# Attention in halves of float16: the low parts of the probabilities against the values' high part alone, two key tiles side by side in TensorE's column halves

## Time and profile before

| | us |
|---|---|
| median of 3 runs | 1426.91 (1426.64 to 1427.55) |
| span of the profiled execution, first to last instruction | 1425.4 |
| busy: PE / PEld / DVE / ACT / POOL | 1318.0 / 838.4 / 1147.2 / 1116.3 / 873.7 |

### The profile page before, as it was taken

The page is one execution under the profiler, slowest core; times in us unless marked ns, Lnnn a source line. Parts: engine busy times, 40 slices in busy tenths (PEclk is TensorE's granted clock), DMA queues, the critical chain, the costliest instruction groups (busy, mean ns, idle before and its releaser), DMA issues. The chain is left out here.

```text
span 1425.4 us, 25329 instructions
## 1 busy us (share of the span) xinstructions
PE 1318.0 (92%) x7328; PEld 838.4 (59%) x7328; DVE 1147.2 (80%) x3062; ACT 1116.3 (78%) x2327; POOL 873.7 (61%) x905
## 2 busy tenths in 40 slices
PE   4689999999999999999999999999999999898886
PEld 2456565665656565665656565666656566565554
DVE  4578887878887888878887888878788787887976
ACT  4768878788888888788887878788887888787664
POOL 1266667386645766386646766387646767786565
PEclk9799999999999999999999999999999999999998
DMA  6101111011101211021101211021100211210002
GB/s 199 27 20 38 64 30 31 27 57 45 37 21 45 59 29 31 23 60 44 36 24 26 72 35 31 23 60 43 38 24 23 75 35 37 61 42 27 18 33 85
DMA packets 45163, 61.82 MB, mean 43 GB/s; under 512 B 10464, under 2 KB 27104, under 8 KB 45024
## 3 DMA queue, kind: packets, MB, share of 16 engines
q1 hardware_dynamic: 45024, 60.20, 14.3%
HBM read 34.74 MB, written 4.46 MB: 27 GB/s over the span
## 5 line engine op out<-in xcount | busy, mean ns | idle before, releaser
L1100 DVE SCALAR_TENSOR_TENSOR prob_lo<-t,prob_hi 128x512 f16<-128x512 f32 x576 | 394.7, 686 | 76.0 <-ACT prob_hi L797 72.2
L797 ACT ACTIVATE prob_hi<-t 128x512 f16<-128x512 f32 x576 | 340.2, 591 | 146.1 <-PE t L1221 140.8
L1165 PE MATMUL s<-k_t,q_t 128*128 128x512 f32 (+3 forms) x1536 | 428.2, 383 | 23.8 <-DVE neg_max L1009 8.5
L829 ACT ACTIVATE prob<-prob,neg_max 128x896 f32<-128x896 f32 (+7 forms) x512 | 392.0, 767 | 7.2 <-DVE neg_max L1009 4.3
L1221 PE MATMUL t<-ident,prob 128*128 128x128 f32 x2304 | 350.8, 275 | 6.9 <-ACT prob L829 6.8
L1221 PEld LDWEIGHTS t<-ident,prob 128*128 128x128 f32 x2304 | 290.6, 143 | 109.7 <-ACT prob L829 13.2
L1009 DVE CUSTOM_DVE_ANT_0 prob<-s,mask 128x512 f32<-128x512 f32 (+3 forms) x512 | 289.6, 583 | 53.4 <-PE s L1165 33.3
L1165 PEld LDWEIGHTS s<-k_t,q_t 128*128 128x128 f32 x1536 | 244.9, 193 | 66.4 <-DVE neg_max L1009 19.0
L1136 PE MATMUL ot<-prob_lo,v_sb 128*128 128x512 f16 x576 | 221.0, 384 | 27.1 <-DVE prob_lo L1100 27.0
L1134 PE MATMUL ot<-prob_hi,v_sb 128*128 128x512 f16 x576 | 223.9, 389 | 0.9 <-DVE o_raw L1081 0.9
L770 POOL TENSOR_TENSOR o_lo<-o_raw,o_hi 128x256 f16<-128x256 f32 x128 | 86.2, 674 | 198.7 <-ACT o_hi L907 196.9
(11 more groups left out here) (106 smaller groups left out, 1841.4 us busy)
## 6 DMA issues: line engine op xcount, KB each, us to landing
swapped<-flat SPq DMA_DIRECT2D x320, 64.0 KB, 2.0
spread<-recip_rows SPq DMA_DIRECT2D x128, 128.0 KB
recip_rows<-turned SPq DMA_DIRECT2D x512, 0.5 KB
raw<-L_attn_w_in SPq DMA_DIRECT2D x8, 768.0 KB, 4.2
raw<-L_attn_w_out SPq DMA_DIRECT2D x8, 512.0 KB, 3.6
out<-acc SPq DMA_DIRECT2D x16, 256.0 KB, 2.0
acc<-L_attn_x SPq DMA_DIRECT2D x3, 1024.0 KB, 10.4
acc<-L_attn_x SPq DMA_DIRECT2D x4, 256.0 KB, 4.2
```

The lines of the kernel that those rows point to most:

```text
L797: act.activation(prob_hi[:, u % 2, :], t_ps[u % 2][:, :], ACT.Copy, scale=P_SCALE).then_inc(prob_hi_done, 1)
L829: act.activation(row, row, ACT.Exp, bias=neg_max[:, kk % 4, h:h + 1], scale=-1.0, accum_out=total[:, kk % 4, h:h + 1]).then_inc(ex_done, 1)
L1100: dve.scalar_tensor_tensor(out=prob_lo[:, u % 2, :], in0=t_ps[u % 2][:, :], scalar=P_SCALE, in1=prob_hi[:, u % 2, :], op0=ALU.mult, op1=AL ...
L1165: mm = pe.matmul(s_ps[:, off:off + cols], q_t[:, h, s * P:(s + 1) * P], k_t[:, part, keys:keys + cols], start=(part == 0), stop=(part == 1))
```

## The change

The matmul with `prob_hi` stays. The one with `prob_lo` is now made for two neighbouring key tiles at once, after the odd one's `prob_hi`: each takes only the 64 columns of the values' high part, the even tile's in rows 0 to 63 of the result, the odd tile's in rows 64 to 127. So the product of the probabilities' low part and the values' low part is left out there. Where a query tile has an odd number of key tiles, its last unit still takes the old matmul of 128 columns. The low parts have four buffers in place of two, and a semaphore of their own, `low_done`.

```diff
@@ buffers and semaphores
+LOWS = 4
-        prob_lo = sb("prob_lo", [P, 2, BANK], F16)
+        prob_lo = sb("prob_lo", [P, LOWS, BANK], F16)
+        low_done = sem("low_done")
@@ ScalarE, o_low
-                            wait(act, pv_done, g, BODY, b * UNITS + first_unit(s + 1))
+                            wait(act, low_done, g, BODY, b * UNITS + first_unit(s + 1))
@@ VectorE, v_sb
-                            wait(dve, pv_done, g, BODY, (b - 1) * UNITS)
+                            wait(dve, low_done, g, BODY, (b - 1) * UNITS)
@@ VectorE, prob_lo
-                        wait(dve, pv_done, g, BODY, u - 1)
-                        dve.scalar_tensor_tensor(out=prob_lo[:, u % 2, :], in0=t_ps[u % 2][:, :], scalar=P_SCALE,
+                        wait(dve, low_done, g, BODY, u - LOWS + 1)
+                        dve.scalar_tensor_tensor(out=prob_lo[:, u % LOWS, :], in0=t_ps[u % 2][:, :], scalar=P_SCALE,
@@ TensorE, values(u)
-                    values_t = v_sb[:, b % 2, j, :]
-                    pe.matmul(ot_ps[k % 2][:, :], values_t, prob_hi[:, u % 2, :], start=(j == 0), stop=False)
-                    wait(pe, prob_lo_done, g, BODY, u + 1)
-                    pe.matmul(ot_ps[k % 2][:, :], values_t, prob_lo[:, u % 2, :], start=False, stop=(j == s)
+                    pe.matmul(ot_ps[k % 2][:, :], v_sb[:, b % 2, j, :], prob_hi[:, u % 2, :], start=(j == 0), stop=False
                               ).then_inc(pv_done, 1)
+
+                    if j % 2:
+                        wait(pe, prob_lo_done, g, BODY, u + 1)
+                        for i in (j - 1, j):
+                            rows = slice(i % 2 * DH, i % 2 * DH + DH)
+                            pe.matmul(ot_ps[k % 2][rows, :], v_sb[:, b % 2, i, 0:DH], prob_lo[:, (u - j + i) % LOWS, :],
+                                      start=False, stop=(j == s)).then_inc(low_done, 1)
+                    elif j == s:
+                        wait(pe, prob_lo_done, g, BODY, u + 1)
+                        pe.matmul(ot_ps[k % 2][:, :], v_sb[:, b % 2, j, :], prob_lo[:, u % LOWS, :], start=False, stop=True
+                                  ).then_inc(low_done, 1)
```

## The result

| | median us | runs | ratio to before (95% interval) |
|---|---|---|---|
| before | 1427.03 | 1426.64 to 1427.55 | |
| changed | 1440.70 | 1438.85 to 1446.82 | 1.0105 (1.0083 to 1.0127) |

The profiled execution has a span of 1439.3 us. The time lies inside the range that was given, 1380 to 1456, but on the other side of 1427 than the 1397 forecast. Of the rivals the drain at a change of shape comes nearest, at 1441 instead of 1457. The granted clock isn't the cause: its mean over the profiled execution is 0.981, and 0.982 before.

A forecast was written before the change was run, and what follows sets the result against it. TensorE was taken as the tightest engine throughout: 256 pairs saving 0.166 us each make 42.5 us, of which 0.7, 29.8 us, comes through. 1425.4 - 29.8 + 1.5 gives 1397 us, range 1380 to 1456.

The forecast's parts named there:

- the drain at a change of shape: Rival: TensorE's array empties before and after each pair, 0.602 us a pair against 0.432, giving 1457 us; chance 0.26.
- Count of pairs and of work elsewhere: 256 pairs and 64 singles on TensorE; work issued by VectorE, ScalarE, GpSimd and SP unchanged by count or shape.
- The halves work at the same time: On TensorE a pair's two matmuls overlap, costing 0.216 us plus the distance between their starts.
- The second start: Distance between a pair's two matmul starts on TensorE, taken as 0.050 us, between 0 and 0.099.
- The price of a pair: On TensorE a pair costs 0.266 us against 0.432, saving 0.166; times 256, 42.5 us, between 30 and 55.3.
- the point where it turns: The prediction is wrong if a pair's two changes of shape on TensorE together cost over 0.166 us.
- The rival with two whole tails: Each pair on TensorE pays two matmul tails of 0.168 us, together 0.336, giving 1457 us; chance 0.26.
- The wait for `prob_lo` moves and costs nothing: For even units TensorE's wait moves from the low product to later turns, ending at the same event; costed at nothing.
- From TensorE's stream to the end, 0.7: 0.7 of TensorE's 42.5 us saving reaches the span, 29.8 us; ends 0.4 and 1.
- The "body" of 157 us: Length of a body after the change, about 157 us, against which VectorE and ScalarE were judged.
- The shares of 84 to 86%: VectorE and ScalarE busy for 84 to 86% of a body after the change, so not bounding it.
- The sum: Span 1425.4 - 29.8 = 1395.6 us, plus 1.5 us for the median, gives 1397 us; ends 1372 and 1415.

The follow-up runs named there:

- experiment 1: The changed kernel with both low products of a pair at full width, same order, waits and four buffers: 1435.6 us, ratio 1.0072.
- experiment 7: The full-width pairs' kernel with the even unit's low product moved ahead of the odd unit's high product: 1428.3 us, ratio 1.0016 to the kernel before.
- experiment 6: The kernel before with the 256 even low products left out, two buffers and all waits kept: 1407.6 us, ratio 0.9881.
- experiment 10: Kernel before without 192 odd low products: 1412.7 us; without 448: 1396.0; without even ones, `prob_lo` short: 1405.8; exponentials short: 1410.9, also without even low products: 1391.7.
- experiment 4: The kernel before with each low product alone in 64 columns of one half, except a query tile's last: 448 stretches, no pair; 1508.7 us, ratio 1.0575.
- experiment 5: The changed kernel with both low products of a pair in the same column half, except a query tile's last pair: 1471.1 us, ratio 1.0315.
- experiment 8: Low products a unit late, against the kernel before: halved pairs behind the next high product 1445.1 us, ahead of it 1436.5; full-width products behind it 1429.1.
- experiment 3: The changed kernel with halved pairs gathered over up to four units, six buffers: 1441.5 us; over a whole query tile, ten buffers: 1440.1 us.
- experiment 9: A query tile's halved pairs in one stretch ahead of its last high product, last one or two units full width: 1441.8 us, 1.0106 to the kernel before.

## Why the prediction was wrong

- **Count of pairs and of work elsewhere: right.** 512 halved matmuls, 64 full ones; VectorE, ScalarE and GpSimd within 0.2% in busy time.
- **The halves work at the same time: right.** The second start was priced at 0.050 us and is 0.003, so the overlap alone was a little better than I took it. That half the columns load in half the time was wrong: the load takes 106 ns, and the second start doesn't wait for it. Without its changes of shape a pair takes 0.216 + 0.003 = 0.219 us by the distances, where I had 0.266.
- **The price of a pair: the step that failed.** I put nothing for going to the halves and back, though I had the rival written down. It is 0.093 us in and 0.118 + 0.056 out, 0.267 in all; a pair costs 0.219 + 0.267 = 0.486 us and not 0.266, against 0.432. The trip is above the 0.166 that I named as the point where it turns. The rival with two whole tails had 0.336, and its 1457 us was too high by that and by the worth below. The tail isn't the most that a change cost, either: the way out to the turns takes 0.118 + 0.056 = 0.174 us, over 0.168. The trace shows that the engine doesn't run on at these changes: the next weight load starts 0.31 us after the high product on the way in and 0.334 us after the pair's second start on the way out, 0.09 and 0.12 us over the 0.216 us that a full-width matmul of 512 columns takes in the stream. On the way in it still starts 0.07 us before the high product's record ends (706.91 against 706.98), so the records, whose ends are modelled, don't show that the array must be empty first; what the engine waits for there is not shown. No row of the kernel before has a change of shape, so my zero rested on nothing measured.
- **The wait for `prob_lo` moves and costs nothing: for the most part wrong.** Matmuls and weight loads taken together, as in the prediction, the turns now wait 18 times, 9.3 us in all. At the even units there were 19.4 us before their low products (a query tile's last units left out), so that part moved and shrank. But before the low products of odd units the wait grew from 45.5 to 64.8 us. The prediction left the odd units as they were, but behind their wait there are two low products now, and at full width that cost 8 us more than one (experiments 1 and 7).
- **From TensorE's stream to the end, 0.7: wrong for savings.** They came through at 0.33 to 0.36, whichever products were left out (experiments 6 and 10). Added stream came through at 0.5 (from experiment 6 to the changed kernel) to 0.7 (experiments 4 and 5), but at a third from experiment 1 to the changed kernel, so one factor does not describe it. I had read the share of the line on the chain as what would be won with it, and it isn't: in experiment 6 the other slots grow by 23.5 us while the shortened ones lose 44.5. (The "body" of 157 us in the prediction is a stretch of 160 us made shorter; a body of 72 units takes 178 us. The shares of 84 to 86% stand.)
- **The sum, with the measured terms:** a pair at no cost for its shape, -19 us (experiment 6); 256 trips, 68 us of stream at 0.48, +33 us; together +14 us, and 13.7 were measured. The second is by difference, so the sum closes by construction; what holds it up are the distances, and experiment 4, where 448 such trips without any pair cost 81 us. By way of experiment 1 it splits otherwise: 10 us for putting the even low product off, at full width, and 5 us for the 14 us of stream that the halves add. That the trips cost is shown; how much of the 13.7 us is theirs hangs on the kernel they are set against.

**Open:** what gives back two thirds of a saving. Neither `prob_lo` on VectorE nor the exponentials on ScalarE does so alone; GpSimd and the transfers, 12% and 7% of the last chain shown, were not relieved. That it is the alternation of many short bounds along the hand-written order is argued from the slots, not shown. Nor do I know why halved pairs ahead of the next high product (experiment 8) cost 9 us at a stream that is the same by the distances.

## What to carry to other kernels

Set the changes of shape against what a stretch in halves saves: here it was 0.27 us for a trip against 0.213 us saved by a lone pair of 512 columns, and 0.216 us by each further one, so a lone pair between full-width matmuls made the stream longer. Gathering up to four pairs spread the trip over more of them and made the slot long, and the long slots were paid in full (experiments 3 and 9: 74 and 79 us longer, for 72 and 76 us of added stream). Before pricing a saving on the busiest engine, leave the work out altogether in one run: that took 19 us of 55 here, and says what the best form of the change can be worth.

## What the chip showed that I had not expected

- Two matmuls in the two column halves start 0.003 us apart, though each weight load lasts 0.106 us; in the same half the first two starts after the change are 0.240 apart and the way out is 0.024 shorter, so the second costs 0.213, against 0.216 for a full-width matmul of 512 columns.
- At each change between 128 and 64 columns the early weight load was gone. That cost 0.093 us on the way in (behind projections as behind high products), 0.120 on the way out to float16 and 0.118 + 0.056 to the float32 turns, whose own loads take 142 ns. It was paid once for a stretch, whether of one pair or of four (0.503, 0.719, 0.934 and 1.150 us in experiment 3).
- A weight load of 64 float16 columns lasts 106 ns, and one of 128 columns 98 ns: half the columns take no less time, at these two shapes.
